# Second attention: high and low parts of the queries stacked on the 128 rows, two score matmuls a head in place of four, and key pieces written in longer runs

## The chip, the cores and the metric

One core of one Trainium2 chip runs the whole program. The metric is the device time in microseconds (us) of one execution. The engines are TensorE (PE in the profile; PEld is its weight load), VectorE (DVE), ScalarE (ACT), GpSimd (POOL) and SyncE (SP, which here issues the DMAs).

## What is computed

Two blocks of gated cross attention and a gated feed-forward layer, on x of 16 batches x 256 rows x 256 features, with a context of 77 rows a batch. In short:

```
x = x + tanh(g_xattn[0]) * attention_0(layernorm(x), ctx)       # 16 heads of 16
x = x + tanh(g_ffn[0])   * quantised_ffn(layernorm(x))
x = x + tanh(g_xattn[1]) * attention_1(layernorm(x), ctx)       # 8 heads of 64
x = x + tanh(g_ffn[1])   * butterfly_ffn(layernorm(x))

# attention_1
q = split_heads(x @ Wq); k = split_heads(ctx @ Wk); v = split_heads(ctx @ Wv)
sim = einsum('bhid,bhjd->bhij', q, k) * 64 ** -0.5
out = einsum('bhij,bhjd->bhid', softmax(sim), v)
return out_heads_merged @ Wo + bo
```

The change is in attention_1 and in the part of the quantised feed-forward layer that prepares keys and values for it.

## The kernel before

The functions run one after the other: `stacked_attention` (first attention), `quantised_ffn`, `late_attention` (second attention), `butterfly_ffn`. x stays in SBUF (`xres`). A float32 product is made of three passes of a rounded format (`three_passes`, L40 to L42): hi x hi, hi x lo and lo x hi.

**The last phase of `quantised_ffn`** makes, for each batch b of 16, the down projection (`f_d_hi`, 36 matmuls of 256 columns), and beside it what the second attention needs from the context: 12 key pieces (`KEYS`, two a batch at batches 6 to 11; six or four batches of context in 462 or 308 columns) and 10 value tiles (`VALUES_AT`, at batches 12 to 14). ScalarE rounds a key piece into `k_stage` (a view of the tensor `f_z`, two buffers, L2040), VectorE writes its low part beside it (L1975), and SyncE stores both to DRAM (`a_key_spill`, L1883). ScalarE may round piece n only when piece n-2 is stored. Value tiles go the same way through `v_stage` (a view of `f_blocks`, two buffers, L2051) to `a_value_spill` (L1890). ScalarE does the rounding of the down projection's input in the same queue (`f_o_hi`, L2012), and TensorE waits for that by way of `f_o_lo` (L1949). SyncE waits for all key stores before the first value store, and ends the phase with the second half of the values' load (L1899).

**`late_attention`** works in slots. In slot b TensorE does the middle of batch b (scores s0 to s3 of two heads each, products with the values p0 to p3), the front of batch b+1 (xt: transpose x; q0, q1: queries; mx0 to mx3: maxima of the scores; mt: transpose of the maxima) and the back of batch b-1 (at0, at1: transposes of the output; pr0, pr1: projection). The order on each engine is written by hand:

```python
PE_SLOT = "s0 xt s1 p0 q0 at0 q1 p1 at1 mx0 s2 mx1 s3 mx2 p2 mx3 p3 mt pr0 pr1".split()
ACT_SLOT = "s0 xt q0 s1 at0 q1 at1 s2 s3 mt xn".split()
DVE_SLOT = "xt ln q0 at0 q1 mx0 mx1 mx2 at1 mx3 norm pr1".split()
```

A head has 64 features, so two heads share the 128 rows. In `kb` the keys of each head fill its own 64 rows and the rest is zero (the tile is cleared once by GpSimd, L990). For one head the scores are `three_passes` (keys high and low, queries high and low) and one more matmul that subtracts each row's maximum (`a_mt` with `a_pick`, L1200). The maxima come from matmuls of the high parts (L1176, 154 columns, two heads each) and a reduction on VectorE (L1121). ScalarE copies the transposed maxima into `a_mt` (L1048). `norm` (L1076 to L1085) divides by the sums, and `pr1` on VectorE (L1135) adds the projection to x. At the start ScalarE also makes the gate's tanh, copies `pick` and loads the table for exp (L1033 to L1035), behind the first `xn` (L1028).

## Time and profile before

| | us |
|---|---|
| median of 3 runs | 1218.51 (1214.71 to 1220.66) |
| the profiled execution | 1217.83 |
| its span, first to last instruction | 1216.0 |
| TensorE matmul busy | 1029.5 (85%) |
| VectorE busy | 775.6 (64%) |
| ScalarE busy | 596.0 (49%) |
| GpSimd busy | 237.1 (20%) |
| mean granted TensorE clock | 0.92 of full |

The span holds four stages: the first attention up to about 305 us, the quantised feed-forward layer up to 708.9, the second attention from 708.93 to 993.07, the butterfly layer after it. Busy matmul time counts overlapping instructions once, and a matmul's end is modelled, so a busy TensorE isn't one at its peak: the time from the start of one matmul to the start of the next tells more. A row of the timeline shows start, duration, engine, line, operation, tiles, count, and in brackets the idle time before it and what ended it.

### The profile page before, as it was taken

How to read it: one execution, taken by the hardware profiler on the slowest of the kernel's cores; microseconds unless marked ns; L12 is line 12 of the kernel's file. 1: busy time of each engine (PE TensorE's matmuls, PEld its weight loads, DVE VectorE, ACT ScalarE, POOL GpSimd, SP SyncE). 2: the span in 40 equal slices, each digit the busy share in tenths (PEclk: the TensorE clock that was granted, in tenths of full speed). 3: DMA queues.
4: the chain of work that ended last, by engine and by line, in shares of the span. 5: the costliest groups of instructions: out<-in, count | busy, mean ns of one | idle time of the engine just before them, and what ended most of it. 6: DMA issues, size and time to landing. Idle time of an engine off the chain costs nothing. (4 is left out here: it accounts for less than half of the span.)

```text
span 1216.0 us, 20623 instructions
## 1 busy us (share of the span) xinstructions
PE 1029.5 (85%) x7089; PEld 901.9 (74%) x7089; DVE 775.6 (64%) x1556; ACT 596.0 (49%) x1038; POOL 237.1 (20%) x422
## 2 busy tenths in 40 slices
PE   6599999999489988456998828999999957999998
PEld 6477777766378867345888728999999955888888
DVE  5357888863458889799595414555555538676562
ACT  3256666654377699697475323444334314232220
POOL 4313333310176000000042021111111003211110
PEclk9689999997679999686899968999999979999999
DMA  6735445561233177687147740110110020000001
GB/s 191 211 93 131 130 130 130 132 195 32 78 140 139 39 255 252 235 307 262 43 106 95 191 119 12 22 21 21 21 21 21 12 79 1 18 19 18 25 27 36
DMA packets 93078, 121.77 MB, mean 100 GB/s; under 512 B 40390, under 2 KB 71110, under 8 KB 90710
## 3 DMA queue, kind: packets, MB, share of 16 engines
q1 hardware_dynamic: 92710, 119.83, 34.2%
q0 software_dynamic: 304, 1.10, 0.3%
q8 instruction: 38, 0.62, 0.2%
q14 instruction: 26, 0.21, 0.1%
HBM read 71.25 MB, written 47.13 MB: 97 GB/s over the span
## 5 line engine op out<-in xcount | busy, mean ns | idle before, releaser
L40 PE MATMUL bank<-f_xt_hi,f_w_hi 128*128 128x512 f32 x320 | 130.9, 409 | 16.7 <-DMA f_xt_lo<-x_spill 8.8
L41 PE MATMUL bank<-f_xt_lo,f_w_hi 128*128 128x512 f32 x320 | 127.9, 400 | 0.0
L42 PE MATMUL bank<-f_xt_hi,f_w_lo 128*128 128x512 f32 x320 | 127.6, 399 | 0.0
L2377 ACT ACTIVATE f_h<-bank,f_b 128x512 f32<-128x512 f32 x64 | 43.3, 691 | 130.3 <-PE bank L42 80.9
L594 ACT ACTIVATE a_prob<-bank 77x512 f32<-77x512 f32 x128 | 72.8, 592 | 34.4 <-PE bank L758 34.0
L660 DVE TENSOR_REDUCE a_maxima<-bank 128x4 f32<-128x308 f32 x128 | 60.4, 472 | 43.7 <-PE bank L733 43.4
L40 PEld LDWEIGHTS bank<-f_xt_hi,f_w_hi 128*128 128x128 f32 x320 | 61.8, 193 | 33.7 <-DMA f_xt_lo<-x_spill 11.2
L40 PE MATMUL bank<-f_w_hi,f_h_hi 128*128 128x256 f32 x256 | 72.6, 284 | 7.6 <-DVE xres L2332 7.6
L755 PE MATMUL bank<-a_stack,a_kb 96*77 96x256 f32 x256 | 73.9, 310 | 4.7 <-ACT a_mt L587 4.7
L42 PE MATMUL bank<-f_w_hi,f_h_lo 128*128 128x256 f32 x256 | 72.4, 283 | 0.0
L41 PE MATMUL bank<-f_w_lo,f_h_hi 128*128 128x256 f32 x256 | 72.3, 283 | 0.0
L42 PEld LDWEIGHTS bank<-f_xt_hi,f_w_lo 128*128 128x128 f32 x320 | 61.8, 193 | 13.9
L41 PEld LDWEIGHTS bank<-f_xt_lo,f_w_hi 128*128 128x128 f32 x320 | 62.1, 194 | 12.2
L758 PE MATMUL bank<-a_mt,a_pick 128*77 128x256 f32 x256 | 70.0, 295 | 0.0
L733 PEld LDWEIGHTS bank<-a_kb,a_stack 96*128 96x128 f32 x256 | 40.8, 200 | 38.9 <-DVE a_maxima L660 28.4
L1055 ACT ACTIVATE a_prob<-bank 77x512 f32<-77x512 f32 x64 | 37.9, 592 | 61.9 <-PE bank L1200 61.9
L733 PE MATMUL bank<-a_kb,a_stack 96*128 96x156 f32 x256 | 58.1, 310 | 9.4 <-DVE a_maxima L660 4.4
L1215 PE MATMUL bank<-a_values,a_prob 77*128 (+1 forms) x512 | 65.8, 272 | 0.0
L40 PE MATMUL bank<-f_d_hi,f_o_hi 128*128 128x256 f32 x192 | 57.6, 300 | 8.8 <-DVE f_o_lo L1949 8.8
L1493 DVE TENSOR_REDUCE f_gmax<-f_hid 128x1 f32<-128x1024 f32 x48 | 55.6, 1212 | 14.0 <-ACT f_hid L1607 13.8
L1215 PEld LDWEIGHTS bank<-a_values,a_prob 77*128 77x128 f32 x512 | 63.0, 193 | 0.0
L40 PE MATMUL bank<-a_wo_hi,a_at_hi 128*128 128x256 f32 x192 | 59.0, 307 | 2.8 <-DVE a_at_lo L664 1.4
(290 smaller groups left out, 3149.3 us busy)
## 6 DMA issues: line engine op xcount, KB each, us to landing
u_spill<-f_ubuf SPq DMA_DIRECT2D x48, 256.0 KB, 2.4
f_uback<-u_spill SPq DMA_DIRECT2D x24, 512.0 KB, 5.5
a_stack<-a_queries SPq DMA_DIRECT2D x16, 512.0 KB, 4.9
f_mats<-in_low_steps SPq DMA_DIRECT2D x12, 512.0 KB, 6.7
a_kb<-a_key_spill SPq DMA_DIRECT2D x32, 154.0 KB, 3.2
xres<-in_x SPq DMA_DIRECT2D x16, 256.0 KB, 4.2
a_queries<-a_q_hi SPq DMA_DIRECT2D x16, 256.0 KB, 2.6
a_queries<-a_q_lo SPq DMA_DIRECT2D x16, 256.0 KB, 2.8
```

The lines of the kernel that those rows point to most:

```text
L40: nc.tensor.matmul(out, w_hi, m_hi, start=start, stop=False)
L41: nc.tensor.matmul(out, w_hi, m_lo, start=False, stop=False)
L42: return nc.tensor.matmul(out, w_lo, m_hi, start=False, stop=stop)
L594: act.activation(prob[0:S, n % 4, :, :].rearrange("p a b -> p (a b)"), (S0, S1)[n % 2][0:S, :], ACT.Exp, scale=SCALE).then_inc(probs, 1)
L660: dve.tensor_reduce(maxima[:, t, 4 * k:4 * k + 4], MX[:, 0:4 * SE].rearrange("p (h s) -> p h s", s=SE)[:, :, 0:S], AX.X, ALU.max).then_inc ...
L733: last = pe.matmul(MX[:, 2 * n * SE:2 * (n + 1) * SE], stack[0:ROWS, par, pair, t * P:(t + 1) * P], kb[0:ROWS, par, :, pair, :], start=Tru ...
L755: pe.matmul(out, kb[0:ROWS, par, a, pair, 0:S], stack[0:ROWS, par, pair, :], start=True, stop=False)
L758: last = pe.matmul(out, pick[:, 2 * pair + a, 0:S], mt[:, par, :], start=False, stop=True)
L1055: act.activation(prob[0:S, n % 2, :, :].rearrange("p a b -> p (a b)"), (S0, S1)[n % 2][0:S, :], ACT.Exp, scale=SCALE).then_inc(probs, 1)
L1215: last = pe.matmul(out_of(t, h), prob[0:S, n % 2, a, t * P:(t + 1) * P], v, start=True, stop=True)
L1493: dve.tensor_reduce(gmax[:, side, m // 2:m // 2 + 1], hid[:, 2 * g:2 * g + 2, f - 1:f + 1, :], AX.XYZ, op).then_inc(g_maxed, 1)
L2377: act.activation(h[:, n % 2, :], hbank[n % 4][:, :], ACT.Gelu, bias=b1[:, n:n + 1]).then_inc(h_ready, 1)
```

## The change

In the second attention:

- Each head `a` of a pair has a tile `q_both[a]` with the high part of its queries in its own 64 rows and the low part in the other 64, and a tile `q_max[a]` with the high part in its own rows and the transposed maxima in 8 of the other rows. `kb` holds for each head two parts: the high keys in both halves, and the low keys in the own half with the constants -1 that pick the head's maximum in the other. A head's scores are then two matmuls (L1228, L1230) in place of four. SyncE copies the high part from `q_both` to `q_max` (step `qm`, 2 DMAs a batch). ScalarE and VectorE make the queries' parts in two instructions of 64 rows in place of one of 128.
- The maxima are taken from `q_both[a]` and the high keys (high and low queries with high keys), head by head: 16 matmuls of 78 columns a batch in place of 8 of 154.
- ScalarE copies the maxima in 4 instructions a batch in place of 1, the first two for head pair 0.
- The orders of the slots are new: `xt` and its copy now begin a slot, and use bank X0; `pr0` stands before mx3. GpSimd adds the bias in the slot of the batch itself (`xb`).
- The keys of a batch come in 6 DMAs in place of 2. Of `kb` only 4 columns are cleared. The gate's work on ScalarE stands before the first `mt`, no longer before the first `xt`, and the -1 constants are loaded in the phase before.

In the last phase of the quantised layer:

- The key pieces are stored as one run of 462 or 308 numbers a row, in place of 6 or 4 runs of 77.
- `v_stage` has three buffers. The wait for the key stores moves from before the first value store to the end of the phase.

```diff
@@ late_tensors
-    late["k_dram"] = nc.dram_tensor("a1_key_spill", (P, B, 2, C, S), F32, kind="Internal").ap()
+    late["k_dram"] = nc.dram_tensor("a1_key_spill", (P, 2, C, B * S), F32, kind="Internal").ap()
@@ late_attention
-        PE_SLOT = "s0 xt s1 p0 q0 at0 q1 p1 at1 mx0 s2 mx1 s3 mx2 p2 mx3 p3 mt pr0 pr1".split()
-        ACT_SLOT = "s0 xt q0 s1 at0 q1 at1 s2 s3 mt xn".split()
-        DVE_SLOT = "xt ln q0 at0 q1 mx0 mx1 mx2 at1 mx3 norm pr1".split()
-        POOL_SLOT = "ln xn".split()
-        SP_SLOT = "kb".split()
+        PE_SLOT = "xt s0 s1 q0 q1 s2 p0 at0 p1 mx0 at1 s3 mx1 p2 mx2 pr0 mx3 p3 mt pr1".split()
+        ACT_SLOT = "xt s0 s1 q0 q1 at0 s2 xn at1 s3 mt".split()
+        DVE_SLOT = "xt ln q0 q1 at0 mx0 mx1 at1 mx2 mx3 norm pr1".split()
+        POOL_SLOT = "ln xb".split()
+        SP_SLOT = "qm kb".split()
...
+                    for a in range(HPC):
+                        sp.dma_start(q_max[a][own[a], par, :, :].bitcast(F32), q_both[a][own[a], par, :, :].bitcast(F32),
+                                     ).then_inc(hi_in[par], 16)
...
+                        for part, rows in ((0, own[a]), (0, across[a]), (1, own[a])):
+                            sp.dma_start(kb[rows, par, a, part, :, 0:S].bitcast(F32),
+                                         late["k_dram"][own[a], part, :, bass.ds(b * S, S)]).then_inc(keys_in[par], 16)
...
-            pool.memset(kb[:].bitcast(F32), 0.0).then_inc(kb_cleared, 1)
+            pool.memset(kb[:, :, :, 0, :, S:SE].bitcast(F32), 0.0).then_inc(kb_cleared, 1)
...
-                    act.activation(mt[0:HEADS, par, :], T0[0:HEADS, 0:T], ACT.Copy).then_inc(mt_copied, 1)
+                    for c0, c1 in ((0, 1), (1, C)):
+                        for a in range(HPC):
+                            last = act.activation(q_max[a][max_rows[a], par, c0:c1, :],
+                                                  T0[0:HEADS, 0:T].unsqueeze(1).to_broadcast([HEADS, c1 - c0, T]),
+                                                  ACT.Copy)
+                        last.then_inc(mt_copied, 1)
...
-                        three_passes(nc, out, kb[:, par, 0, n, a, :], kb[:, par, 1, n, a, :],
-                                     q_hi[:, par, n, :], q_lo[:, par, n, :], True, False)
-
-                        last = pe.matmul(out, pick[:, h, 0:S], mt[:, par, :], start=False, stop=True)
+                        pe.matmul(out, kb[:, par, a, 0, n, 0:S], q_both[a][:, par, n, :], start=True, stop=False)
+
+                        last = pe.matmul(out, kb[:, par, a, 1, n, 0:S], q_max[a][:, par, n, :], start=False, stop=True)
@@ quantised_ffn
+            NSTAGE = 3
...
-                        sp.dma_start(late["k_dram"][:, b0:b0 + nb, part, c, :],
-                                     k_stage[:, n % 2, part, 0:nb * S].bitcast(F32).rearrange("p (b s) -> p b s", s=S),
-                                     ).then_inc(k_saved[n % 2], 16)
+                        sp.dma_start(late["k_dram"][:, part, c, b0 * S:(b0 + nb) * S],
+                                     k_stage[:, n % 2, part, 0:nb * S].bitcast(F32)).then_inc(k_saved[n % 2], 16)
...
                 weight("wo")
-                for n in range(2):
-                    sp.wait_ge(k_saved[n], 16 * NK)
+                sp.wait_ge(ocoded, B)
+                sp.dma_start(late["pick_raw"], late["picks"]).then_inc(late["pick_in"], 16)
                 for i in range(NV):
                     save_values(i)
...
                 fetch_values(1, NV)
+                for n in range(2):
+                    sp.wait_ge(k_saved[n], 16 * NK)
```

How the change moves instructions, at two places. The first is TensorE at the head of a slot in the loop. Before, from behind s0 (L1145 is `xt`, L1204 and L1215 are `p0`; the L40, L41, L42 and L1200 between are s1):

```order
L1145 REGISTER_ALU
L1151 MATMUL bank<-ident,a_xn 128x128 x4
L40 MATMUL bank<-a_q_hi,a_kb 77x256
L41 MATMUL bank<-a_q_lo,a_kb 77x256
L42 MATMUL bank<-a_q_hi,a_kb 77x256
L1200 MATMUL bank<-a_mt,a_pick 77x256
L40 MATMUL bank<-a_q_hi,a_kb 77x256
L41 MATMUL bank<-a_q_lo,a_kb 77x256
L42 MATMUL bank<-a_q_hi,a_kb 77x256
L1200 MATMUL bank<-a_mt,a_pick 77x256
L1204 REGISTER_ALU
L1215 ISA
```

Now, from `xt` (L1177) to the first matmul behind s1, which belongs to q0:

```order
L1177 MATMUL bank<-ident,a_xn 128x128 x4
L1220 ISA
L1222 REGISTER_ALU
L1225 REGISTER_ALU
L1228 MATMUL bank<-a_q_both,a_kb 77x256
L1230 MATMUL bank<-a_q_max,a_kb 77x256
L1228 MATMUL bank<-a_q_both,a_kb 77x256
L1230 MATMUL bank<-a_q_max,a_kb 77x256
L1222 REGISTER_ALU
L1228 MATMUL bank<-a_q_both,a_kb 77x256
L1230 MATMUL bank<-a_q_max,a_kb 77x256
```

What moved: s0 and s1 have half the matmuls, `xt` stands ahead of both, and behind s1 no `p0` stands between the transpose of x and q0.

The second place is SyncE from the key loads of the last phase's end into the second attention. Before:

```order
L1877 DMA a_raw<-in_wo 128x4x256
L1890 DMA a_value_spill<-f_blocks 128x520 x4
L1925 DMA w_spill<-f_y 128x2056
L1890 DMA a_value_spill<-f_blocks 128x520 x2
L1899 DMA a_values<-a_value_spill 77x8x520
L1890 DMA a_value_spill<-f_blocks 128x520 x3
L1890 DMA a_value_spill<-f_blocks 80x520
L1899 DMA a_values<-a_value_spill 77x8x520
L1808 UNCONDITIONAL_BRANCH
L966 UNCONDITIONAL_BRANCH
L968 DMA a_pick_raw<-in_pick 128x624
L969 DMA a_gate_raw<-in_gx 128x1
```

Now:

```order
L1929 DMA a_values<-a_value_spill 77x8x520
L1838 UNCONDITIONAL_BRANCH
L969 UNCONDITIONAL_BRANCH
L993 DMA a_kb<-a_key_spill 64x4x77 x6
L996 DMA a_gate_raw<-in_gx 128x1
L997 DMA a_bo_raw<-in_bo 128x256
L978 DMA a_q_max<-a_q_both 64x1024 x2
```

What moved: the constants are loaded ahead of the value stores, batch 0's keys are the first loads of the second attention, and the gate's inputs come behind them.

## Rows read from the trace of the kernel before

**Rows 1.** Waits from 619 to 709 us: total us, times, longest us.
```profile
ACT f_z L2040 <- DMA a_key_spill<-f_z: 26.4, 8, 5.0
ACT f_blocks L2051 <- DMA a_value_spill<-f_blocks: 18.4, 5, 6.9
```
**Rows 2.** DMA issues from 620 to 712 us: KB each, median us to landing.
```profile
a_key_spill<-f_z SPq DMA_DIRECT2D x16, 231.0 KB, 6.5
...
a_value_spill<-f_blocks SPq DMA_DIRECT2D x9, 260.0 KB, 3.0
```
**Rows 3.** Timeline, 635 to 687 us: ScalarE behind a store, TensorE's two longest stalls.
```profile
649.44 0.56 ACT L2040 ACTIVATE f_z<-bank 128x462 fp32r<-128x462 f32 x1 [2.78 <-DMA a_key_spill<-f_z]
...
656.41 0.39 PE L40 MATMUL bank<-f_d_hi,f_o_hi 128*128 128x256 f32 x1 [2.81 <-DVE f_o_lo L1949]
...
686.03 0.47 PE L40 MATMUL bank<-a_wv_hi,a_c_hi 128*128 128x512 f32 x1 [2.72 <-ACT f_blocks L2051]
```
**Rows 4.** Windows: stretch, span, busy (count) by engine, granted clock, DMA share, GB/s.
```profile
657.00:661.00 4.00, 4.00 (x24) 4.00 (x22) 2.38 (x5) 3.52 (x9) 0.00 (x0) 0.57 0.55 103
```
**Rows 5.** Timeline of the phase's end, 696 to 710 us.
```profile
700.46 0.88 DVE L1956 SCALAR_TENSOR_TENSOR xres<-bank,f_back,xres 128x256 f32<-128x256 f32 x2 [2.78 <-PE bank L42]
703.46 1.28 ACT L2051 ACTIVATE f_blocks<-bank 128x512 f32<-128x512 f32 x2 [6.19 <-DMA a_value_spill<-f_blocks]
706.83 0.32 SPq L1899 DMA_DIRECT2D a_values<-a_value_spill  x1
708.93 2.15 POOL L990 MEMSET a_kb<- 128x2464 f32 x1 [41.34 <-POOLq L48]
```
**Rows 6.** Timeline, start of the second attention: ScalarE's gate work and q0.
```profile
717.89 0.20 ACT L1033 ACTIVATE a_tg<-a_gate_raw 128x1 f32<-128x1 f32 x1 [3.63 <-DMA a_bo_raw<-in_bo]
...
721.49 0.58 PE L40 MATMUL bank<-a_xt_hi,a_wq_hi 128*128 128x256 f32 x1 [6.06 <-DVE a_xt_lo L1107]
```
**Rows 7.** Windows, one slot in the loop (columns as rows 4).
```profile
779.82:795.57 15.75, 15.54 (x136) 15.28 (x135) 8.97 (x24) 6.39 (x12) 2.67 (x6) 1.00 0.10 20
```
**Rows 8.** Timeline, TensorE's weight loads in a slot: xt, s1, and p0 behind it.
```profile
844.59 0.48 PEld L1151 LDWEIGHTS bank<-ident,a_xn 128*128 128x128 f32 x4
...
845.04 0.15 PEld L40 LDWEIGHTS bank<-a_q_hi,a_kb 128*77 128x77 f32 x1
...
845.98 0.97 PEld L1215 LDWEIGHTS bank<-a_values,a_prob 77*128 77x128 f32 x8
```
**Rows 9.** Timeline, 575 to 583 us: the matmuls with the fewest columns.
```profile
579.52 1.84 PE L2128 MATMUL bank<-f_y,f_blocks 128*128 128x1 f32 x16
```
**Rows 10.** Timeline of a slot: mt, norm's ends, the maxima's copy, pr1, xt's low part, q0's copy.
```profile
840.70 0.38 PE L1183 MATMUL bank<-ident,a_maxima 128*8 128x128 f32 x2
...
840.90 0.21 DVE L1076 RECIPROCAL a_rden<-bank 128x7 f32<-128x7 f32 x1 [0.40 <-PE bank L1215]
...
841.12 0.37 ACT L1048 ACTIVATE a_mt<-bank 8x256 fp32r<-8x256 f32 x1 [1.81 <-PE bank L1183]
...
842.58 0.28 DVE L1085 TENSOR_SCALAR a_att<-bank,a_rden 128x64 f32<-128x64 f32 x1
...
844.09 0.88 DVE L1135 SCALAR_TENSOR_TENSOR xres<-bank,a_tg,xres 128x256 f32 x2 [1.23 <-PE bank L42]
...
846.10 0.69 DVE L1107 TENSOR_TENSOR a_xt_lo<-bank,a_xt_hi 128x512 fp32r<-128x512 f32 x1 [1.13 <-ACT a_xt_hi L1038]
...
848.62 0.60 ACT L1042 ACTIVATE a_q_hi<-bank 128x512 fp32r<-128x512 f32 x1 [2.55 <-PE bank L42]
```
**Rows 11.** The key loads' line: issue ns min/median/max, and time to landing.
```profile
L982 SPq DMA_DIRECT2D a_kb<-a_key_spill x32: 596/599/2447, 711.1 to 949.4; - x32
...
DMA to landing us min/median/max: 2.9/3.2/7.2
```
**Rows 12.** TensorE alone by windows: stretch, span, busy (count), clock, DMA share, GB/s.
```profile
273.00:274.00 1.00, 0.51 (x6) 1.00 0.85 238
...
276.00:277.00 1.00, 1.00 (x7) 0.50 0.90 190
```

More of the change, by code:

```diff
@@ L1008, in step @@
                     pool.tensor_tensor(nmr[:], nmean[:], rstd[:], ALU.mult).then_inc(ln_nmr, 1)
-                elif what == "xn":
+                    if isinstance(b, int) and b == 0:
+                        for a in range(HPC):
+                            pool.memset(q_max[a][:].bitcast(F32), 0.0).then_inc(mt_cleared, 1)
+                elif what == "xb":
                     if isinstance(b, int) and b == 0:
@@ L1928, in _ @@
                 fetch_values(1, NV)
+                for n in range(2):
+                    sp.wait_ge(k_saved[n], 16 * NK)
                 sp.wait_ge(z_stored, 16)
```

164 lines of the change are left out of this document (91 added, 73 removed).

## The prediction

> **What bounds the kernel now.** I read the chain that ended last, the slices and the windows by stage first, then two stages more closely: the last phase of the quantised layer, and the second attention.
>
> In the last phase TensorE has work for most of the time, and what stops it comes from stores. ScalarE waited 26.4 us in 8 pieces for key stores and 18.4 us in 5 pieces for value stores [rows 1]. A key store of 231 KB takes 6.5 us to land (median), a value store of 260 KB takes 3.0 [rows 2]: the keys go in runs of 77 numbers, the values in runs of 520. ScalarE's queue is in order, so behind such a wait (649.44) stands the rounding that TensorE's next batch needs, and TensorE idles 2.81 us at 656.41; a value buffer that isn't free gives 2.72 us at 686.03 [rows 3]. After the first of these the clock was low, 0.57 over the next 4 us, that is mostly at 1.2 GHz: 24 matmuls ran there [rows 4]. At the end VectorE's last addition starts at 700.46, as TensorE's last matmul releases it, and ends at 701.34, but ScalarE gets its last value buffer only at 703.46, SyncE issues the last load at 706.83, and the second attention starts at 708.93 [rows 5].
>
> In the second attention TensorE bounds the loop. A slot takes 15.75 us with 15.54 us of matmuls, at full clock [rows 7]; the other engines are busy for 9 us or less. So a matmul that goes is worth its spacing, until another engine's queue becomes the longer way round. The spacing is start to start: 8 score matmuls of 256 columns from 845.04 to 845.98, 0.1175 us each; 4 transposes from 844.59 to 845.04, 0.11 each [rows 8]; 16 matmuls of one column in 1.84 us, 0.115 each [rows 9].
>
> **The last phase of the quantised layer.** The key stores become runs of 462 or 308 numbers. I take a landing near that of the value stores, about 2.5 to 3 us [rows 2]; the bounds are 3.0 and the old 6.5. A batch's two key pieces come some 6 us after the two before them, and two pieces are four stores: at 3 us, overlapping, they are done in time; at 6.5 they aren't. A key piece is rounded before its two stores and needs the buffer of the piece before last. So the stall of 2.81 goes, and with it the low clock behind it. There 24 matmuls took 4 us, which at 0.1175 us each [rows 8] is 2.8: 1.2 us. The value tiles no longer start behind a wait for all key stores and have a third buffer, so the 2.72 goes [rows 3]. Together 6.7 us. What is late next is TensorE itself.
>
> The end of the phase: ScalarE's last value copies no longer wait for stores, so the last to end is VectorE's addition, 0.9 us behind TensorE's last matmul; from SyncE's last issue (706.83) to the start of the next function it took 2.1 us [rows 5], which I keep. That gives 3.0 us where there are 8.5 (700.46 to 708.93): 5.5 us. The moved load of the constants and the half megabytes of weights stand earlier in SyncE's queue and are hidden by key and down-projection work; the 2.6 MB of value stores and 2.5 MB of value loads now lie in less time, for which I take 0.7 us off. Sum of the phase: **-11.5 us**. Bounds: -5.5 (the end isn't gained, or the key stores still hold ScalarE) and -13.5 (the small stalls go too).
>
> **The start of the second attention.** Before q0 TensorE idles 6.06 us [rows 6], because ScalarE's copy of x transposed stands behind the gate's inputs (717.89), a copy of `pick` and a table load. Now that copy needs only itself (0.6) and VectorE's low part (0.69) with handovers, some 1.5 us: -4.6. The clearing of `kb`, 2.15 us on GpSimd ahead of the layer norm's steps [rows 5], shrinks to 4 columns of each piece: -2.0. Against it: the queries' parts in two instructions each, +0.5 on ScalarE and +0.6 on VectorE; four groups of maxima with two more matmuls each, at the low clock that holds there, 8 x 0.23 = +1.8 (nothing covers them, since each group waits for VectorE); the maxima's four copies, +0.3 before s0. The two copies of the constants on ScalarE lie beside the layer norm. Batch 0's six key loads, 0.6 us of issue each and up to 7.2 to landing [rows 11], are in by some 11 us from the start, before mx0 at some 14. Sum: **-3.3 us**; bounds -6 and +1 (keys late).
>
> **A slot of the loop.** Removed: 16 score matmuls of 256 columns, 16 x 0.1175 = -1.88 us. Added: 8 matmuls for the maxima, since 8 of 154 columns become 16 of 78. This size isn't in the trace; it lies between one column (0.115) and 256 (0.1175), so a shorter matmul isn't a cheaper one: +0.92. The Trainium skill, TensorE: Matmul & The Clock Gate, Back-to-back issue gap, has pairs of load and matmul at 128 columns 81 ns apart; by that the sixteen would cost 1.3 us in place of 1.84, and the slot would gain 0.5 us more. The row with one column contradicts it here.
>
> New stalls, at three places.
> - *q0 behind xt.* Count from the start of mt (840.70 in the old slot) [rows 10]. TensorE: mt 0.22, pr1 12 x 0.1175 = 1.41, xt 0.45, s0 and s1 0.47 each: free for q0 at 3.02. VectorE: norm starts 0.20 after mt does and takes 1.96 (840.90 to 842.86), then pr1 0.88, then xt's low part 0.69: 3.73, and q0 can start at 3.85. ScalarE: the copies start at 0.42 (841.12); two of 256 columns at 0.37 and two of 768, which from 0.37 for 256 and 0.60 for 512 I estimate at 0.83, partly overlapping, some 2.0 in all; then xt's copy 0.6, ready at 3.05, hence tied with norm and pr1. Stall: **0.8**, up to 1.2 if the copies don't overlap. In the old order p0 and s1's four more matmuls lay between, and there is no such stall.
> - *at1 behind at0's parts.* Copy 0.60, low part 0.69 and handovers, 1.65; TensorE has p1 and mx0 meanwhile, 0.9 + 0.46: **0.3**.
> - *mx0 behind q1's parts, and pr0 behind at1's*: 1.1 us more in the parts against s2, p0, at0, p1 in between: **0.2** together, where mx0's old stall was 0.3.
>
> Sum of a slot: -1.88 + 0.92 + 1.3 - 0.35 = 0.0 us. So the gain in matmuls is given back as waits: a slot stays at 15.7, to -0.1. Over 14 slots: **-0.7 us**. Bounds: -0.96 a slot if no stall comes (-13 in all), +0.5 a slot if all are at their longest (+7). SyncE issues 8 DMAs a slot at 0.6 [rows 11], 4.8 of 15.7 us; `q_max`'s own half is copied some 9 us before s0 needs it. The last slots, where each step waits for the one before, keep their length.
>
> **Sum.** 1217.83 (the profiled execution, 1.8 above its span, 0.7 below the median of the runs) - 11.5 - 3.3 - 0.7 = 1202.3; against the median 1203.
>
> **Rivals.**
> - *The loop is cheaper than I count*: 78 columns cost less than one column's row says, or VectorE and ScalarE overlap more. TensorE then binds again and the slot loses up to 1 us: 1203 - 13 = 1190. For it: 0.8 us of stall is a difference of two sums of 3 to 4 us, so 0.3 less in each is easy. Against: both chains, over VectorE and ScalarE, give the same end. The skill's 81 ns lead the same way. Chance 0.13.
> - *The stores don't shorten* (the landing is set by bytes and by what else is in flight, not by the run), or the squeezed value stores hold the phase's end. Then -5.5 there: 1209. For it: even with long runs ScalarE waited 18.4 us for value stores [rows 1]. Against: the value stores with their long runs land in 3.0 [rows 2]. Chance 0.14.
> - *The clock falls in the loop.* The place is the stall before q0 with the transposes ahead of it, in every slot. In the first attention the clock went to 1.2 GHz by 276 us though TensorE was never idle for long, only 0.51 busy at 273 [rows 12]. A fall that holds for 4 us costs some 2 to 3 us. From 6 falls on the gain of 15 is gone, and with one in each of 14 slots it is +35: 1238. Against: at 0.8 us TensorE stays near 0.92 busy in a slot. The page named above (What's actually happening) puts the low level behind idle time; by it alone this couldn't happen, but rows 12 decide. Chance 0.06.
>
> **How the numbers follow.** The forecast has 0.67. Its own range is 1196 to 1210, the terms' bounds taken half together. To hold 8 in 10, the range reaches to 1192 and 1213, into the first two rivals; left out are the lower half of the first, the third, and tails. A measurement of this kernel can tell about 0.5% from no change, 6 us, so faster means under 1212.4 (the forecast's upper end and part of the second rival lie above): most of the forecast, the first rival and most of the second, 0.85; within 0.5% 0.08; slower 0.07.
>
> **What would show it.** Right: no wait of ScalarE on key stores, their landing under 3.5 us; the second attention starts at 696 to 699; from there to q0 about 7 us, not 12.6; 126 matmuls in a slot of 15.6 to 15.8 with a stall of about 0.8 before q0, released by xt's low part; clock 1.00 in the loop. Wrong: a slot under 15.2 (the stalls were counted too high) or over 16.2, a start of the second attention after 702, or a clock under 0.95 in the loop.

## The result and the profile after

| | before, us | changed, us | ratio, 95% interval |
|---|---|---|---|
| first measurement: 4 runs of each | 1219.59 | 1204.10 (1203.44 to 1206.98) | 0.9881 [0.9843, 0.9919] |
| second, in a later session: 17 and 12 runs | 1213.16 | 1213.79 (1209.17 to 1217.14) | 0.9999 [0.9976, 1.0022] |

The forecast was 1203 us, and the first measurement gave 1204.1. But the second, longer one shows no difference at all. Which of the two has the reasons on its side is read from the stages. The record has the second on chip 2 and doesn't say where the first ran. The ratios are the record's own, made from all the runs, and can lie 0.2% off the quotient of two medians. One execution of e5_short, 1211.94 us, was 1.6% above the fastest of its kernel and is left out of that ratio.

**Last phase of the quantised layer.** The changed kernel's profiled execution takes 1206.98 us, its span 1205.2. It was already 4.1 us ahead at the store of z, before any changed work (614.65 us before, 610.52 after), so stages are compared, not clock readings. Waits, 615 to 690 us, changed kernel (total us, times, longest us):

```profile
ACT f_z L2072 <- DMA a_key_spill<-f_z: 9.0, 8, 4.1
ACT f_blocks L2083 <- DMA a_value_spill<-f_blocks: 3.6, 1, 3.6
```

and the DMA issues of the same stretch (KB each, median us to landing):

```profile
a_key_spill<-f_z SPq DMA_DIRECT2D x16, 231.0 KB, 2.4
...
a_value_spill<-f_blocks SPq DMA_DIRECT2D x9, 260.0 KB, 5.6
a_key_spill<-f_z SPq DMA_DIRECT2D x8, 154.0 KB, 2.0
```

The eight key waits remain, but make 9.0 us for 26.4, and value waits 3.6 for 18.4 [rows 1]. A key store of 231 KB lands in 2.4 us, median of 16, for 6.5 [rows 2]; the value stores, now closer together, take 5.6 for 3.0. TensorE's stalls at 656.41 and 686.03 [rows 3] and the low clock between them [rows 4] have no counterpart. The end of the phase and the start of the second attention, timeline (start, duration, engine, line, operation, tiles, count, idle time before it):

```profile
685.10 0.59 ACT L2083 ACTIVATE f_blocks<-bank 80x512 f32<-80x512 f32 x1 [3.61 <-DMA a_value_spill<-f_blocks]
686.58 0.88 DVE L1988 SCALAR_TENSOR_TENSOR xres<-bank,f_back,xres 128x256 f32<-128x256 f32 x2 [7.57 <-PE bank L42]
687.71 0.32 SPq L1929 DMA_DIRECT2D a_values<-a_value_spill  x1
689.88 0.13 POOL L1003 MEMSET a_kb<- 128x16 f32 x1 [35.09 <-POOLq L48]
...
695.69 0.69 DVE L1131 TENSOR_TENSOR a_xt_lo<-bank,a_xt_hi 128x512 fp32r<-128x512 f32 x1 [4.52 <-ACT a_xt_hi L1052]
...
696.43 0.58 PE L40 MATMUL bank<-a_xt_hi,a_wq_hi 128*128 128x256 f32 x1 [1.41 <-DVE a_xt_lo L1131]
```

From VectorE's last addition to the second attention's start it is 3.3 us for 8.5 [rows 5], from there to q0 6.55 us for 12.56 [rows 6].

**The loop.** Windows by stage, changed kernel (stretch, us, busy and count for TensorE, its weight load, VectorE, ScalarE and GpSimd, granted clock, DMA share, GB/s):

```profile
718.00:724.00 6.00, 5.37 (x45) 5.02 (x45) 3.24 (x5) 4.44 (x8) 1.13 (x2) 0.99 0.32 76
724.00:726.00 2.00, 1.96 (x14) 1.81 (x13) 0.48 (x2) 0.10 (x1) 0.00 (x0) 0.72 0.38 88
726.00:738.00 12.00, 10.82 (x47) 9.60 (x48) 4.73 (x16) 5.08 (x9) 2.68 (x6) 0.50 0.16 31
738.00:754.00 16.00, 15.15 (x124) 14.37 (x124) 10.00 (x25) 8.48 (x16) 0.94 (x3) 0.98 0.30 65
...
863.86:880.06 16.20, 15.26 (x126) 14.49 (x126) 10.25 (x26) 9.28 (x18) 2.68 (x6) 1.00 0.28 62
```

A slot is 16.20 us with 15.26 of matmuls, for 15.75 with 15.54 [rows 7]: fewer matmuls, more waiting. And after the clock had risen to 2.4 GHz at 718, it fell again to 1.2 GHz, from 725 to 738. In one slot of the loop, timeline:

```profile
861.55 2.40 ACT L1069 ACTIVATE a_q_max<-bank 8x256 fp32r<-8x256 f32 x4 [4.13 <-PE bank L1212]
863.86 0.57 ACT L1052 ACTIVATE a_xt_hi<-bank 128x512 fp32r<-128x512 f32 x1
...
863.20 0.86 DVE L1161 SCALAR_TENSOR_TENSOR xres<-bank,a_tg,xres 128x256 f32 x2
864.46 0.69 DVE L1131 TENSOR_TENSOR a_xt_lo<-bank,a_xt_hi 128x512 fp32r<-128x512 f32 x1 [0.39 <-ACT a_xt_hi L1052]
...
864.00 0.34 PE L1228 MATMUL bank<-a_q_both,a_kb 128*77 128x256 f32 x1 [0.15 <-ACT a_q_max L1069]
865.28 0.38 PE L40 MATMUL bank<-a_xt_hi,a_wq_hi 128*128 128x256 f32 x1 [0.59 <-DVE a_xt_lo L1131]
```

ScalarE's four copies of the maxima take 2.4 us, the copy of x transposed stands right behind them, VectorE, done with pr1 at 864.06, waits 0.39 us for it, and TensorE waits before s1 (for the copies) and before q0 (for the low part).

**Stages of each kernel.** The columns: from the issue of the store of z (line 1912 before, 1942 after) to the second attention's first instruction; the second attention from there to the start of its last two additions into `xres`; the distance of two low parts of x transposed in the loop; and how often the clock fell from the fourth slot on (without the low stretches that every kernel has in the last 20 us of this stage). Each is of the one profiled execution; the kernel before has only the one from the first measurement.

| kernel | z store to second attention | second attention | slot | falls in the loop | ratio to before |
|---|---|---|---|---|---|
| before | 94.3 | 283.3 | 15.70 | 0 | |
| changed, first | 79.4 | 294.0 | 16.19 | 0 | 0.9881 |
| changed, second | 79.6 | 297.9 | 16.19 | 1 | 0.9999 |
| e1_phase | 78.6 | 282.4 | 15.70 | 0 | 0.9894 |
| e2_runs | 82.3 | 282.0 | 15.70 | 0 | 0.9920 |
| e4_late | 103.6 | 292.0 | 16.19 | 0 | 1.0170 |
| e7_orig | 96.3 | 298.3 | 16.18 | 1 | 1.0133 |
| e5_short | 79.8 | 294.9 | 15.78 | 2 | 0.9867 |
| e6_order | 79.6 | 284.5 | 15.35 | 1 | 0.9867 |
| e9_swap | 80.0 | 297.8 | 16.19 | 1 | 0.9962 |
| e10_both | 79.2 | 285.0 | 15.36 | 1 | 0.9898 |
| e12_fill | 79.3 | 275.1 | 15.05 | 0 | 0.9814 |
| e8_start | 79.5 | 277.3 | 15.70 | 0 | 0.9823 |
| e11_burst | 80.2 | 277.3 | 15.70 | 0 | 0.9843 |

So the phase gives 15 us, and the second attention, forecast to give 4 more, costs 10.7 us in the first profile and 14.6 in the second.

### The profile page after: what moved, and what is told of

Its sections match the earlier page's. It is cut to its first block and busy times, and to the rows that moved or that the text cites. A ratio compares the mean times of both kernels' runs of the same rounds, so it can differ in the third digit from the quotient of the medians.

```text
span 1205.2 us, 20734 instructions
## 1 busy us (share of the span) xinstructions
PE 1024.8 (85%) x6961; PEld 890.7 (74%) x6961; DVE 795.8 (66%) x1588; ACT 643.7 (53%) x1119; POOL 237.9 (20%) x423
## 5 line engine op out<-in xcount | busy, mean ns | idle before, releaser
L40 PE MATMUL bank<-f_xt_hi,f_w_hi 128*128 128x512 f32 x320 | 129.7, 405 | 16.1 <-DMA f_xt_lo<-x_spill 9.3
L41 PE MATMUL bank<-f_xt_lo,f_w_hi 128*128 128x512 f32 x320 | 126.9, 397 | 0.0
L42 PE MATMUL bank<-f_xt_hi,f_w_lo 128*128 128x512 f32 x320 | 126.9, 396 | 0.0
L2409 ACT ACTIVATE f_h<-bank,f_b 128x512 f32<-128x512 f32 x64 | 43.3, 691 | 129.5 <-PE bank L42 79.5
L594 ACT ACTIVATE a_prob<-bank 77x512 f32<-77x512 f32 x128 | 72.6, 592 | 30.6 <-PE bank L758 30.1
L660 DVE TENSOR_REDUCE a_maxima<-bank 128x4 f32<-128x308 f32 x128 | 60.5, 473 | 42.6 <-PE bank L733 42.3
L40 PEld LDWEIGHTS bank<-f_xt_hi,f_w_hi 128*128 128x128 f32 x320 | 61.3, 192 | 32.8 <-DMA f_xt_lo<-x_spill 11.9
L40 PE MATMUL bank<-f_w_hi,f_h_hi 128*128 128x256 f32 x256 | 72.8, 285 | 7.6 <-DVE xres L2364 7.6
L1069 ACT ACTIVATE a_q_max<-bank 8x256 fp32r<-8x256 f32 (+1 forms) x64 | 37.6, 587 | 70.4 <-PE bank L1212 69.6
L755 PE MATMUL bank<-a_stack,a_kb 96*77 96x256 f32 x256 | 70.1, 297 | 4.5 <-ACT a_mt L587 4.5
L42 PE MATMUL bank<-f_w_hi,f_h_lo 128*128 128x256 f32 x256 | 72.2, 282 | 0.0
L41 PE MATMUL bank<-f_w_lo,f_h_hi 128*128 128x256 f32 x256 | 72.1, 282 | 0.0
L42 PEld LDWEIGHTS bank<-f_xt_hi,f_w_lo 128*128 128x128 f32 x320 | 61.1, 191 | 13.7
L41 PEld LDWEIGHTS bank<-f_xt_lo,f_w_hi 128*128 128x128 f32 x320 | 61.4, 192 | 12.1
L1140 DVE TENSOR_TENSOR a_q_both<-bank,a_q_both 64x512 fp32r<-64x512 f32 x64 | 44.1, 689 | 38.9 <-ACT a_q_both L1057 37.8
L758 PE MATMUL bank<-a_mt,a_pick 128*77 128x256 f32 x256 | 66.7, 284 | 0.0
L40 PE MATMUL bank<-a_wo_hi,a_at_hi 128*128 128x256 f32 x192 | 61.0, 318 | 2.9 <-DVE a_at_lo L664 1.4
```

The source lines that it names most:

```text
L40: nc.tensor.matmul(out, w_hi, m_hi, start=start, stop=False)
L41: nc.tensor.matmul(out, w_hi, m_lo, start=False, stop=False)
L42: return nc.tensor.matmul(out, w_lo, m_hi, start=False, stop=stop)
L594: act.activation(prob[0:S, n % 4, :, :].rearrange("p a b -> p (a b)"), (S0, S1)[n % 2][0:S, :], ACT.Exp, scale=SCALE).then_inc(probs, 1)
L660: dve.tensor_reduce(maxima[:, t, 4 * k:4 * k + 4], MX[:, 0:4 * SE].rearrange("p (h s) -> p h s", s=SE)[:, :, 0:S], AX.X, ALU.max).then_inc ...
L755: pe.matmul(out, kb[0:ROWS, par, a, pair, 0:S], stack[0:ROWS, par, pair, :], start=True, stop=False)
```

## The experiments

### e1_phase: the phase's part alone

```diff
-    late["k_dram"] = nc.dram_tensor("a1_key_spill", (P, B, 2, C, S), F32, kind="Internal").ap()
+    late["k_dram"] = nc.dram_tensor("a1_key_spill", (P, 2, C, B * S), F32, kind="Internal").ap()
...
+            NSTAGE = 3
...
-                for n in range(2):
-                    sp.wait_ge(k_saved[n], 16 * NK)
...
+                for n in range(2):
+                    sp.wait_ge(k_saved[n], 16 * NK)
```

(The wait for the key stores moves to the phase's end. The stores, as under e2_runs, and the loads follow the layout.)

> The kernel before with the change to the quantised layer's last phase alone (key pieces stored in longer runs, three value buffers, the wait for the key stores at the phase's end); the second attention is as before, its loads read the new layout. My theory, as the traces of before and after read: this part gives 14.9 us (the second attention starts 19.05 us earlier after the change, 4.2 of which were already there before the phase), so 1205 against 1219.6, ratio 0.988, and the second attention, with its old code, takes as long as before, 284 us. Rival A, the prediction's terms: 11.5 us, 1208. Rival B: part of the 14.9 belongs to the second attention's own edits (the clearing of its key buffers, the order of its first steps) and the phase's part alone gives 10 us or less, 1210 or more.

Measured: 1197.53 us for 1212.85, 0.9894 [0.9840, 0.9949]. The phase is 15.7 us shorter, the second attention as before. By the stages my theory holds: the phase's gain doesn't need the second attention's edits, and 11.5 was too small. The time alone can't tell: its interval takes in the theory and both rivals.

### e2_runs: long key runs alone

```diff
-                        sp.dma_start(late["k_dram"][:, b0:b0 + nb, part, c, :],
-                                     k_stage[:, n % 2, part, 0:nb * S].bitcast(F32).rearrange("p (b s) -> p b s", s=S),
-                                     ).then_inc(k_saved[n % 2], 16)
+                        sp.dma_start(late["k_dram"][:, part, c, b0 * S:(b0 + nb) * S],
+                                     k_stage[:, n % 2, part, 0:nb * S].bitcast(F32)).then_inc(k_saved[n % 2], 16)
```

(The spill's layout and its loads are those of e1_phase.)

> The kernel before with the longer runs of the key stores alone; two value buffers and the early wait for the key stores stay. Theory (the stall of 2.81 us at 656.41 and the low clock behind it came from key stores that land late): the key stores land in 2.4 to 3 us, ScalarE no longer waits for them, those 4.0 us go, but the 2.72 us for a value buffer at 686.03 and most of the 8.5 us at the phase's end stay: -4 to -6 us, 1214 to 1216. Rival: the long runs alone give nearly all of the phase's gain, since the late value stores and the late end only followed from the late key stores: -11 to -15 us, 1205 to 1209.

Measured: 1203.67 us, 0.9920 [0.9891, 0.9948], or -9.7 us; by the stages -12.0 in the phase. The rival holds by the stages; the time lies between it and the theory, and the interval leaves the theory out. The waits of e2_runs, 620 to 699 us:

```profile
ACT f_blocks L2050 <- DMA a_value_spill<-f_blocks: 17.3, 4, 7.4
ACT f_z L2039 <- DMA a_key_spill<-f_z: 8.2, 8, 3.3
```

ScalarE still waits 17.3 us for value buffers, nearly as long as before the change, and yet TensorE has no stall of over 0.3 us left between 621 us and the phase's end (the kernel before has four, 7.2 us in all): its last matmul there starts 75.6 us after z's store issue, for 85.5 in the kernel before. So the stall of 2.72 us that I gave to the missing third value buffer [rows 3] needs no third buffer to go: it goes with the late keys. The third buffer and the late wait give the rest, at the phase's end: from TensorE's last matmul start to the second attention it is 6.7 us in e2_runs, 4.4 in e1_phase. The third buffer alone wasn't tried.

### e4_late and e7_orig: the second attention's part alone

```diff
-    late["k_dram"] = nc.dram_tensor("a1_key_spill", (P, 2, C, B * S), F32, kind="Internal").ap()
+    SK = S + 1
+    late["k_dram"] = nc.dram_tensor("a1_key_spill", (P, 2, C, B, SK), F32, kind="Internal").ap()
...
-            NSTAGE = 3
```

(The two value buffers and the early wait for the key stores come back; the constants stay loaded in the phase.)

> The changed kernel with the quantised layer's last phase as it was: the second attention's change alone. Prediction's terms: start -3.3 and loop -0.7, so -4 us, 1215.6. Theory from the profile after: the start gives about 5 to 6 us (12.56 to 6.55 from the start to q0, GpSimd's clearing 2.15 to 0.13, which lies in that stretch, against longer groups of maxima), but the slot is 16.2 us for 15.7, +0.49 over 14 slots = +6.9, so +1 to +4 us, 1221 to 1224, ratio 1.00. Rival: the slot is 16.2 only because something of the new phase reaches into it (key loads of short pieces, order of the weights); then here the slot is 15.7 and the time 1213 to 1216.

Measured: 1233.44 us, 1.0170 [1.0128, 1.0211]: 20 us slower, which neither theory had. The second attention is 8.7 us longer, as read; but the phase is also 9.3 us longer. ScalarE waits a little more for stores than in the kernel before (26.4 and 18.4 us there [rows 1]):

```profile
ACT f_z L2073 <- DMA a_key_spill<-f_z: 27.1, 8, 4.9
ACT f_blocks L2084 <- DMA a_value_spill<-f_blocks: 21.9, 4, 9.8
```

and the clock was 0.57 in this stretch of the phase:

```profile
646.00:656.00 10.00, 3.54 (x13) 3.19 (x14) 4.75 (x6) 5.68 (x11) 0.00 (x0) 0.57 0.85 88
```

My "old" spill wasn't the old one: it put the runs of 77 numbers of a row at a pitch of 78, where in the kernel before they lie 616 numbers apart. e7_orig takes the layout of the kernel before:

```diff
+    late["k_dram"] = nc.dram_tensor("a1_key_spill", (P, B, 2, C, S), F32, kind="Internal").ap()
...
+                                         late["k_dram"][own[a], bass.ds(b, 1), part, :, :].rearrange("p o c s -> p (o c) s")
```

> The second attention's change alone, as e4_late, but with the key spill exactly as in the kernel before (batch first, runs of 77 numbers in the old places; the old buffers and waits). e4_late had a pitch of 78 numbers in its spill, its key stores took 7.5 us to land for 6.5, and its phase was 9.3 us longer than in the kernel before. Theory (that was the pitch of the spill, an artefact of e4_late; the second attention's change costs 9 us by itself): the phase is as before, 94 us from the store of z to the second attention's start, second attention 292 us for 283, +8 to +10 us, ratio 1.007. Rival (the longer phase belongs to the moved loads and not to the pitch): +17 to +20 us, ratio 1.015.

Measured: 1230.87 us for 1213.16, 1.0133 [1.0097, 1.0170]. The stages say which part of each theory stands: the phase is 96.3 us, 2.0 over the kernel before, so the other layout had made most of the 9.3 us (its pitch and its order of axes weren't tried apart), as far as one profile of each tells; but the second attention has a slot of 22.1 us and comes to 298.3, 15 over. So the measured +16 to +18 us lies nearer the rival's number, and its cause, a longer phase, is 2.0 us of it at most. The second attention's change then costs 8.7 to 10.7 us without a fall in the loop (e4_late and the first profile), and 14.6 to 15.0 with one (the second profile and e7_orig). The two halves also speak on the two measurements: 0.9894 for the phase alone times 1.0133 for the second attention alone is 1.003, near the second (0.9999) and far from the first (0.9881).

### e5_short: shorter copies of the maxima

```diff
-                    for c0, c1 in ((0, 1), (1, C)):
+                    for c0, c1 in ((0, 1), (1, 2)):
```

> The changed kernel, with the second of the two copies of the maxima for each half 256 columns long instead of 768 (the scores of the head pairs 2 and 3 are then not shifted by the maxima of this batch: that part is left out). Theory (the slot is bound through ScalarE there: four copies of the maxima, 2.39 us, then the copy of x transposed 0.57 us, then VectorE's low part 0.69, then q0): the copies end 0.85 us earlier, the wait before s1 goes and q0 comes earlier until VectorE's own chain of norm and pr1 holds it, so a slot of 15.7 to 15.9 for 16.2 and -4 to -7 us against the changed kernel, 1197 to 1200. Rival (VectorE's norm, pr1 and low part take as long by themselves, so that ScalarE's copies only end together with them): the slot stays at 16.1 or more, -1 us or less.

Measured: 1197.55 us for 1212.85 without the slowest, 0.9867 [0.9816, 0.9919]; the four lie at 1192.5 to 1211.9. The copies take 1.53 us for 2.40 and the slot 15.78 for 16.19: -0.41, as the theory has it. ScalarE's copies do bind the slot. The profiled execution is the slowest of the four, and its windows show where a good part of the spread comes from:

```profile
786.00:787.00 1.00, 0.88 (x8) 0.74 (x7) 0.95 (x3) 1.00 (x3) 0.00 (x0) 1.00 0.52 111
787.00:788.00 1.00, 0.82 (x7) 0.74 (x7) 0.93 (x2) 0.92 (x2) 0.00 (x0) 0.93 0.86 160
788.00:801.00 13.00, 13.00 (x64) 12.91 (x63) 4.06 (x13) 2.68 (x6) 0.00 (x0) 0.50 0.22 56
801.00:802.00 1.00, 1.00 (x8) 1.00 (x7) 0.77 (x2) 0.38 (x1) 0.00 (x0) 0.75 0.00 0
...
951.00:952.00 1.00, 0.84 (x6) 0.75 (x7) 0.97 (x2) 0.00 (x0) 0.00 (x0) 0.85 0.87 164
952.00:965.00 13.00, 13.00 (x64) 12.91 (x63) 3.96 (x13) 2.68 (x6) 0.00 (x0) 0.50 0.06 19
```

In the midst of the loop, with TensorE 0.8 to 0.9 busy, the clock goes to 1.2 GHz for some 13 us. That slot takes 22.05 us: 6.3 more. A second fall, at 951.7, lies in the last slot and shows only in the stretch behind the last low part, 42.6 us for 36.6 to 37.1 in most of the changed form. The two make some 12 of the 19 us between the fastest and the slowest run.

### after_again: the changed kernel once more

> The changed kernel itself, once more, beside the others. By stages in the profiles so far: the phase of the quantised layer -15, the second attention +8.7 to +10.6 (its start to the first low part of x transposed 11.8 to 5.8 us; its first three slots 55.4 us for 46.8, with a second fall of the clock to 1.2 GHz some 8 us after it had risen; 12 slots of 16.19 for 15.70; its tail 36.6 to 38.4 for 36.2). Theory (what the stages sum to is all there is): -4 to -6 us, ratio 0.995 to 0.997. Rival (the first measurement, 0.988, holds, and another stage also gained): -12 to -15 us, ratio 0.988 to 0.990.

Measured: 1213.79 us for 1213.16, 0.9999 [0.9976, 1.0022]. Closest to the theory that the stages are all there is, and a little slower still: here too a fall lies in the loop, in a slot of 22.01 us for 16.19, 5.8 more:

```profile
761.00:763.00 2.00, 1.70 (x15) 1.48 (x14) 1.95 (x4) 1.96 (x4) 0.00 (x0) 1.00 0.68 131
763.00:776.00 13.00, 13.00 (x64) 12.91 (x63) 4.07 (x13) 3.64 (x7) 0.00 (x0) 0.50 0.24 57
```

By the stages -14.7 + 14.6 = -0.1 us. (The profiled executions are above the medians of this measurement in both kernels: 1217.14 for 1213.79 here, and 1217.83, of the first measurement, for 1213.16.) The mean clock is 0.911 to 0.920 over the 12 runs, 0.922 to 0.926 in the four of the first measurement; the kernel before has 0.923 on average in the second. So the changed kernel loses clock in the second measurement and not in the first. That the first chip or those four runs had fewer falls fits this, but only one of the four has a profile here; what decides it stays open.

### e6_order: x transposed at the slot's end

```diff
-        PE_SLOT = "xt s0 s1 q0 q1 s2 p0 at0 p1 mx0 at1 s3 mx1 p2 mx2 pr0 mx3 p3 mt pr1".split()
-        ACT_SLOT = "xt s0 s1 q0 q1 at0 s2 xn at1 s3 mt".split()
-        DVE_SLOT = "xt ln q0 q1 at0 mx0 mx1 at1 mx2 mx3 norm pr1".split()
+        PE_SLOT = "s0 q0 s1 q1 s2 p0 at0 p1 mx0 at1 s3 mx1 p2 mx2 pr0 mx3 p3 mt xt pr1".split()
+        ACT_SLOT = "s0 q0 s1 q1 at0 s2 xn at1 s3 mt xt mb".split()
+        DVE_SLOT = "ln q0 q1 at0 mx0 mx1 at1 mx2 mx3 norm xt pr1".split()
```

(`mb` is the copies for the last three head pairs.)

> The changed kernel with another order of the steps: the transposes of x for the batch after next at the slot's end, before pr1, so that their rounding and low part are long done when q0 comes; the queries' banks exchanged; the maxima's copies of the last three head pairs after xt's copy. Theory (a slot of 16.19 us holds 0.74 us of waiting before q0, 0.3 before s1 and the slow restarts behind them): the slot is 15.0 to 15.4 us, 12 of them give 10 to 14 us, 1189 to 1195 where the changed kernel has 1200 to 1204. Rival A (VectorE's and ScalarE's chain of maxima, norm, pr1 and copies round the slot binds at 16): -3 us or less. Rival B (the clock falls in the loop as it did once in e5_short, for 13.6 us at a cost of 6.3 us a time): the slots in between are short, single slots are 21 to 22 us.

Measured: 1196.87 us, 0.9867 [0.9842, 0.9892]. The slot is 15.35 us, so the theory of the two waits holds for it; the time is a little above its range of 1189 to 1195. One slot of 20.1 us, with one of 16.5 behind it, stands among them, rival B's: together 6.0 us more.

### e9_swap, e10_both, e11_burst: is it the transfer?

In each profile with a fall from the fourth slot on, it came within 1 us of the start of at1, and in the first ones also with the transfer into `q_max`. e9_swap (and e10_both on e6_order):

```diff
-                    sp.wait_ge(q_rounded, (b + 1) * NP)
+                    if isinstance(b, int) and b == 0:
+                        sp.wait_ge(q_rounded, NP)
+                    else:
+                        sp.wait_ge(scores, b * HP)
```

e11_burst, on e8_start:

```diff
-        SP_SLOT = "kb".split()
+        SP_SLOT = "qm kb".split()
...
+                        sp.dma_start(burst[a][rows, par, :, :].bitcast(F32),
+                                     q_hi[rows, par, :, :].bitcast(F32)).then_inc(bursts[par], 16)
```

> The changed kernel, with the copy of the queries' own half into q_max (two DMAs of 256 KB a slot, 190 to 290 GB/s for some 2 us) issued only after the scores of the slot's last head pair, some 2.5 us later, beside mx1 to mx3 and pr0. In the profiles of the changed form so far the clock fell to 1.2 GHz in five loop slots of six profiles (e5_short 787.9, after_again 763.4, e6_order 879.9, e7_orig 745 to 757 as all of them in the second slot, and 958), each time within 1 us of this transfer, where TensorE is also 0.7 to 0.9 busy ahead of at1; the form before (four profiles) has none in the loop. Theory 1 (the transfer, together with all other engines at work, brings the fall about): no fall at this place, the low second slot goes too, mean clock 0.920 or more for 0.915, and -4 to -9 us against the changed kernel (ratio 0.993 to 0.996). Theory 2 (TensorE's short waits ahead of at1 do it, and the transfer only happens to be there): falls at the same place, mean clock 0.915, ratio 1.000 as after_again.

> e6_order (transposes of x at the slot's end) with q_max's transfer moved as in e9_swap. Theory 1 (transfer brings the falls about): the slots stay at 15.34 us, none of 20 to 22, the second slot is no longer lengthened: -4 to -9 us against e6_order, ratio to before 0.979 to 0.983, level with e8_start. Theory 2 (TensorE's waits do it): as e6_order, 0.987.

> e8_start (the old second attention, the new phase and the new order of the first steps) with two DMAs of 256 KB a slot added at the place where the changed kernel has them, from the rounded queries into buffers that nothing reads; s0 waits for them, some 10 us later. Theory 1 (the transfer alone brings the clock's falls about): slots of 21 to 22 us in the loop, mean clock 0.915 for 0.929, +5 to +10 us against e8_start. Theory 2 (TensorE's waits do it; this slot is 99% busy): no falls, at most +1 us, ratio to before 0.982 to 0.984. Between them (both are wanted together): as theory 2 here, but e9_swap as theory 1.

Measured: e9_swap 1208.19 us for 1212.13, 0.9962 [0.9937, 0.9988]; e10_both 0.9898 [0.9853, 0.9944]; e11_burst 0.9843 [0.9807, 0.9878]. The windows of e9_swap at its fall:

```profile
759.00:760.00 1.00, 0.88 (x8) 0.74 (x6) 0.97 (x2) 1.00 (x3) 0.00 (x0) 1.00 0.00 0
760.00:761.00 1.00, 0.82 (x7) 0.74 (x6) 0.63 (x2) 0.61 (x2) 0.00 (x0) 0.78 0.03 8
761.00:774.00 13.00, 13.00 (x64) 12.91 (x62) 4.38 (x14) 3.53 (x6) 0.00 (x0) 0.50 0.36 77
```

No transfer runs in the two us ahead of the fall, and with it added to the old loop (e11_burst) none came in the profile. So the transfer isn't needed for a fall, and in that one profile it wasn't enough: as the one cause, theory 1 falls by the traces. The times are less clear. e9_swap is a little faster than after_again, though the intervals overlap, and its mean clock of 0.919 lies between theory 2's 0.915 and theory 1's 0.920; e10_both is, if anything, slower than e6_order, at 0.917 for 0.918. That the transfer makes falls more frequent isn't ruled out. TensorE at the fall, timelines of e9_swap and of e6_order:

```profile
760.29 0.84 PE L1262 MATMUL bank<-ident,a_att 128*128 128x128 f32 x4 [0.18 <-DVE a_at_lo L1156]
```

```profile
879.83 1.06 PE L1264 MATMUL bank<-ident,a_att 128*128 128x128 f32 x4 [0.18 <-DVE a_at_lo L1158]
```

It is the same step in all seven falls from the fourth slot on: the four transposes of at1, behind a wait shown as 0.16 to 0.18 us, with a wait before mx0 just ahead. The fall in the second slot, which all profiles of the new form have, isn't at that step, since that slot has no at1. There a wait of 0.55 to 0.57 us before mx0 lies 0.9 to 2.8 us ahead; in the changed kernel's first profile the fall is at 724.9 and the wait here:

```profile
722.36 0.61 PE L1206 MATMUL bank<-a_kb,a_q_both 128*128 128x78 f32 x4 [0.56 <-issue]
```

Waits are thus near every one of these falls; that they bring them about was only tried once, in e12_fill.

### e12_fill: the waits before mx0 and at1 filled

```diff
-        PE_SLOT = "s0 q0 s1 q1 s2 p0 at0 p1 mx0 at1 s3 mx1 p2 mx2 pr0 mx3 p3 mt xt pr1".split()
+        PE_SLOT = "s0 q0 s1 q1 s2 p0 at0 p1 s3 mx0 at1 mx1 p2 mx2 pr0 mx3 p3 mt xt pr1".split()
```

> e6_order with one step of TensorE moved: the scores of the last head pair (s3, 0.47 us) ahead of mx0 and at1 and not behind them, so that they fill the waits there (0.28 us before mx0, 0.18 before at1, and the slow restarts behind them), the place at which the clock fell in six of seven profiles of the changed form, with the transfer (e7_orig, after_again) or without it (e9_swap: no DMA within a us of the fall at 760.8). Theory (TensorE's short waits at that place bring the fall about): no fall there, mean clock 0.925 or more for 0.918, the second slot no longer lengthened, and the slot 15.0 to 15.2 us for 15.34: -8 to -15 us against e6_order, ratio to before 0.974 to 0.980. Rival (what matters is the kind of work there, few columns a matmul, not the waits): the slot is 0.2 to 0.3 us shorter, but falls come as before: -3 to -5 us, ratio 0.983 to 0.985.

(The count in that text is one short: there were eight profiles of the changed form by then.)

Measured: 1189.44 us for 1211.21, 0.9814 [0.9788, 0.9841], between the theory's range and the rival's. The slot is 15.05 us, with TensorE busy nearly through:

```profile
845.00:860.30 15.30, 15.14 (x129) 14.63 (x128) 10.42 (x26) 9.64 (x19) 2.66 (x6) 1.00 0.30 69
```

There is no fall in the loop of this profile, but the second slot is lengthened as in all of the new form, and the mean clock of the six runs is 0.921, not 0.925. Three of the nine profiles of the new form have no fall from the fourth slot on, so one more without says little. Five of them lie at 1186 to 1190 us and one at 1195.9, about one fall away. So filling the waits helps, and that it ends the falls isn't shown.

### e8_start: the old second attention with the new order of its first steps

This is e1_phase with one more edit:

```diff
-            pool.memset(kb[:].bitcast(F32), 0.0).then_inc(kb_cleared, 1)
...
+                    if isinstance(b, int) and b == 0:
+                        pool.memset(kb[:].bitcast(F32), 0.0).then_inc(kb_cleared, 1)
...
-                        act.activation(tg[:], gate_raw[:], ACT.Tanh).then_inc(g_done, 1)
-                        act.activation(pick[:], pick_raw[:], ACT.Copy).then_inc(picked, 1)
-                        act.activation(warm[:], gate_raw[:], ACT.Exp)
...
+                        act.activation(tg[:], gate_raw[:], ACT.Tanh).then_inc(g_done, 1)
+                        act.activation(pick[:], pick_raw[:], ACT.Copy).then_inc(picked, 1)
+                        act.activation(warm[:], gate_raw[:], ACT.Exp)
```

(The three ScalarE lines now stand ahead of the first copy of the maxima; the bias that needs the gate is added a slot later, as in the changed kernel.)

> e1_phase (the kernel before with the change to the last phase alone) and, of the second attention's change, only the order of its first steps: the gate's tanh, the copy of pick and the table load stand behind the copy of x transposed, and GpSimd clears the key buffers after the first layer norm and not ahead of it. The 16 score matmuls more and the slot of 15.7 us stay. Theory: from the start of the second attention to xt's low part 6 us for 11.4, nothing given back, so 277 us for 282.4 and -5 us against e1_phase, -18 to -20 us against before, ratio 0.984 to 0.985: faster than the changed kernel. Rival (what is gained before q0 is waited away in the first two slots, on maxima or keys or at a clock that stays low longer, as in the changed kernel): no more than -2 us against e1_phase, ratio 0.988 or more.

Measured: 1192.65 us for 1213.16, 0.9823 [0.9795, 0.9852]. The second attention takes 277.3 us, as expected, and its first slots (16.6 and 14.5 us) are those of the kernel before: nothing is given back. Level with e12_fill (which ran on another chip, 4 for 2), it beats both kernels, with all 16 score matmuls a slot kept.

## Why the prediction was right in its number and wrong in its reasons

- **The phase: forecast -11.5, measured -14.7 to -15.7.** The mechanism is as told. The step that failed is the sum of "together 6.7 us": it stopped at the two long stalls and one low stretch, while from z's store to TensorE's last matmul the changed kernel's phase is 9.7 us shorter. "The small stalls go too", which stood only in the bound, was the case: 1.22 us at 665.38 and 0.46 at 673.22 were among them. With these it is 8.4 us; the remaining 1.3 isn't traced. I had said that no wait on key stores would be left; 9.0 us are, and hold up nothing. The end came as told: 5.2 us for 5.5.
- **The start: forecast -3.3.** The gate work and the clearing gave 6.0 us up to q0, for 6.6 told. The first slot then gave 2.3 back; the eight matmuls and longer parts had 3.2. What was missing is a further fall of the clock, 725 to 738 us: the second and third slots take 18.24 and 18.41 us for 14.56 and 15.74. Of these 6.3 us some 1.0 is the longer slot, and 5.3 the fall. All nine profiles of the new form have it. The five of the old form also have two low stretches up to the second slot (to 739.1 us in the kernel before), but none behind them.
- **The slot: forecast 0.0 to -0.1, measured +0.49,** the bound given for the case that all stalls are at their longest. I had 1.3 us of stalls and 2.0 for the copies. The copies take 2.4, q0 comes 4.15 us behind mt, not 3.85, and the stalls add to 1.7 (counted from where the next matmul could have started: 0.74 before q0, 0.31 before s1, where I had none, 0.28 before mx0, 0.36 before at1). Against that, a matmul of 78 columns costs less than I took: the four of mx1 take 0.09 us each up to the next step (872.82 to 873.18):

```profile
872.82 0.54 PE L1206 MATMUL bank<-a_kb,a_q_both 128*128 128x78 f32 x4
873.18 0.64 PE L1245 MATMUL bank<-a_values,a_prob 77*128 x4
```

  so the row with one column [rows 9] was no guide. The trace of the kernel before had a better one: its two matmuls of 154 columns take 0.09 each too.

```profile
853.15 0.35 PE L1176 MATMUL bank<-a_kb,a_q_hi 128*128 128x154 f32 x2
853.33 0.29 PE L40 MATMUL bank<-a_q_hi,a_kb 128*77 128x256 f32 x1
```

  The Trainium skill (TensorE: Matmul & The Clock Gate, Back-to-back issue gap), with 81 ns at 128 columns, was also nearer. The first rival had 78 columns cheaper, and 1190 us from it. The cheaper matmuls came, but the gain didn't, since ScalarE and VectorE held the slot (e5_short, e6_order).

  Step by step through one slot of each kernel, from mt to mt (840.70 to 856.45, and 861.13 to 877.34): the scores give -1.89 us, the maxima +0.63 where I had +0.92, the stalls with the slow first matmuls behind them +1.85 for 1.3, the old stalls that went -0.46 for -0.35. A further +0.32 is spread over the projections, values and transposes of the output, whose matmuls are the same and which the sum took as unchanged. Together that is +0.45 us. So the terms that failed are the stalls, by 0.55, and these places between the steps, put at nothing.
- **The rival "the clock falls in the loop", chance 0.06, was the one that mattered.** I priced a fall at 2 to 3 us, "that holds for 4 us". It holds for some 13 us and costs 5.8 to 6.3. Six of the nine profiles of the new form have one from the fourth slot on. I looked for it before q0, where the long stall is; it came at at1, behind waits of 0.2 us. Rows 12 had shown a fall near a stretch with TensorE half busy, and I gave them too little weight. What brings a fall about stays open.
- **Sum.** The terms had -11.5 - 3.3 - 0.7. They are -15, +4.8 in the first profile (-6.0 + 2.3 + 6.3 for the start and its slots, and 2.2 in the tail of the last batch, where most others of the new form have 0.4 to 0.9), +5.9 for twelve slots of 0.49, and about +6 for each fall in the loop. That makes -4 without one and +2 with one. The second measurement, +0.6, agrees with it. The first has -15.5; its profiled pair has -10.8 in the span, of which 4.1 lie ahead of the changed work and 2.4 behind the second attention, where nothing was changed. So the number came out right by luck: a phase that gave more than forecast, a second attention that cost where a gain was forecast, and help from stages that the change doesn't touch. In the second measurement the forecast of "faster" isn't borne out. Of the signs that the prediction named, a slot of 15.6 to 15.8 us and no wait on key stores failed; the landing, the stall of 0.8 us before q0 and the 7 us up to it held.

## What to carry to other kernels

Read what a removed matmul is worth from the other engines' way round the slot first: 16 score matmuls of a slot went for 8 short ones, and the slot grew, until the order of the steps was changed (16.19 to 15.05 us). Stores in longer runs gave 10 to 12 us with a change of layout alone, and a stall blamed on a missing buffer went with them. Time a change in two sessions and with a dozen runs before a gain of 1% is believed, and add up the stages of a profile: here they gave -4 when four runs said -15.
